# One field of every third tile fetched row by row by SyncE in place of a gather of GpSimd

## The chip, the cores and the metric

The kernel runs on one core of one Trainium2 chip. The metric is the time of one execution on the device, in microseconds (us). The engines are TensorE (PE; its weight loads are PEld), VectorE (DVE), ScalarE (ACT), GpSimd (POOL) and SyncE (SP). The kernel before takes 558.92 us, the median of three runs (558.09 to 559.47).

## The reference

2048 samples each carry 32 field indices. Every index picks a row of 256 floats from the table of its field. The kernel computes the dot products of all pairs of the 32 rows, appends 16 given numbers, and sends the result through three dense layers.

```python
e = jnp.stack([tbl_0[ids[:, 0]], ..., tbl_31[ids[:, 31]]], axis=1)   # [2048, 32, 256]
dots = jnp.einsum('bnd,bmd->bnm', e, e)
z = dots[:, iu, ju]                                # 496 pairs i < j
h = jnp.concatenate([z, dense_ctx], axis=1)        # 512 features
h = jnp.maximum(h @ W_top1 + b_top1, 0.0)          # 512 -> 512
h = jnp.maximum(h @ W_top2 + b_top2, 0.0)          # 512 -> 256
y = h @ W_top3                                     # 256 -> 1
```

The 12 largest tables have 12500 rows, the others 1250 or 1000. All is float32.

## The kernel before

The samples go in 16 tiles of 128, numbered 0 to 15. For six of the small fields (1000 rows each) a row is looked up by TensorE, as a product of a one-hot matrix with a table that is kept on the core (`look_up`, L346). The row numbers for these arrive by `load_ids` (L251, issued by SP), DVE makes the one-hot matrices (`make_one_hot`, L725), and each look-up serves two tiles. There are three such look-ups in each step of one tile.

The other 26 fields are gathered. They stand in 13 pairs per tile, called units; tile 0 has two more units, since half of its looked-up fields are gathered too. For each unit POOL issues two indirect DMAs (`gather`, L303), each of which reads 128 rows of 1 KB by a list of 128 row numbers. They land in one of nine places of the ring `rows` (`PLACES = 9`); before a gather POOL waits for `turn_done`, which says that the unit nine earlier was turned. TensorE turns a unit (`turn`, L330): it waits for `gathered[place]`, transposes the four 128x128 blocks into a bank of PSUM, and ACT or DVE copies them into `turned`.

A step of tile t on TensorE begins with `turn_all(t)`: units 4 to 12 of the tile, with `turn_features(t - 1)` (L412, it raises `ft_done`) after unit 6, and then the first layer of the tile before (L427). It goes on with `gram(t, k)` (L368) in eight parts, between which stand the parts of the look-ups, the second layer of the tile before (L448) and the first four units of tile t + 1. Unit 12, the last of a tile, is thus the last that TensorE turns ahead of the tile's products, and it holds fields 30 and 31 of the kernel's own numbering.

SP issues the plain loads in program order. After the loads of the start it runs one loop turn per tile: three `load_ids`, each behind a wait for `one_hot_made` (a ring of three buffers), and one `load_dense` behind a wait for `ft_done`. An instruction that waits on SP holds all that stands behind it.

The last tile has its own products (`last_gram`, L389), and after them come the last layers and the output of 2048 numbers (L291).

Of the kernel before, what the change touches and what calls it, by code (L numbers as in the profile page):

```python
# [35 lines left out]
    return np.array(order)  # L36


def dlrm_tower(nc, dense_ctx, ids, small_ids, tables, w1, b1, w2, b2, w3, out):
    fp32 = mybir.dt.float32  # L40
    fp32r = mybir.dt.float32r
    int32 = mybir.dt.int32
# [23 lines left out]
        BEGIN.append(len(UNITS))  # L66

    PLACES = 9

    ACT_UNITS = [0, 2, 4, 6, 8, 10, 12]  # L70
    RING = 4
# [42 lines left out]
    with ctx:  # L114
# [6 lines left out]
        def sem(name):  # L121
            return ctx.enter_context(nc.semaphore(name))
# [40 lines left out]
        late_h2 = turn_ps[1]  # L163

        weighted = area[:, 3 * FEATURES:3 * FEATURES + HIDDEN2]

        y_rows = area[0:TILES, 0:P]

# [9 lines left out]
        dense_in = sem("dense_in")  # L178
        weights_in = sem("weights_in")
        table_in = [sem(f"table_in{i}") for i in range(SMALL)]  # L180
        gathered = [sem(f"gathered{i}") for i in range(PLACES)]
        row_numbers_ready = sem("row_numbers_ready")
        ident_zero = sem("ident_zero")
# [50 lines left out]

        def n_gathered(n):

            return 16 * sum(len(UNITS[m][1]) for m in range(n % PLACES, n + 1, PLACES))

        def n_ids(n):

# [4 lines left out]
        @block.sync  # L245
        def _(sp):
            def load_ids(n):
                f, t, tiles = LOOKUPS[n]
                if n >= IDS_RING:
                    sp.wait_ge(one_hot_made, n - IDS_RING + 1)  # L250
                sp.dma_start(ids_across[:, n % IDS_RING, 0:tiles * P],  # L251
                             small_ids[f, t * P:(t + tiles) * P].partition_broadcast(P),
                             ).then_inc(ids_across_in[n % IDS_RING], 16)

            def load_table(i):
                table = tables[i].rearrange("(p r) d -> p r d", r=SUB)
                sp.dma_start(landed[0:SP_WIDE, i, :, 1, :], table[0:SP_WIDE, :, :]).then_inc(table_in[i], 16)
                sp.dma_start(landed[SP_WIDE:SP, i, :, 1, :], table[SP_WIDE:SP, :, :]).then_inc(table_in[i], 16)

            def load_dense(t):  # L260
                if t > 0:
                    sp.wait_ge(ft_done, t)
                sp.dma_start(features[:, PAIRS:FEATURES], dense_ctx[t * P:(t + 1) * P, :]).then_inc(dense_in, 16)

            sp.dma_start(row_ids[:, 0, :], ids[:, 0, :]).then_inc(row_ids_in[0], 16)
# [12 lines left out]
            sp.dma_start(w3_sb[:, :], w3.rearrange("n a -> (a n)").partition_broadcast(P)).then_inc(weights_in, 16)  # L278
            sp.dma_start(b1_sb[:, :], b1).then_inc(weights_in, 16)
            sp.dma_start(b2_sb[:, :], b2.partition_broadcast(P)).then_inc(weights_in, 16)  # L280
            for c in range(KC):
                sp.dma_start(w1_sb[:, c, :], w1[c * P:(c + 1) * P, :]).then_inc(weights_in, 16)
            load_ids(5)
            for t in range(TILES):
                if t + 2 in FIRST:
                    for n in range(FIRST[t + 1], FIRST[t + 2]):
                        load_ids(n)
                if t + 1 < TILES:
                    load_dense(t + 1)
            sp.wait_ge(y_kept, 1)  # L290
            sp.dma_start(out.rearrange("(t p) a -> t (p a)", p=P), y_rows).then_inc(y_out, 16)  # L291
            sp.wait_ge(y_out, 16)

        @block.gpsimd
        def _(pool):
            def gather(n):
# [2 lines left out]
                    pool.wait_ge(row_ids_in[t], 16)  # L299
                if n >= PLACES:  # L300
                    pool.wait_ge(turn_done, n - PLACES + 1)
                for j, f in enumerate(unit):
                    pool.indirect_dma_start(  # L303
                        out=rows[:, n % PLACES, j, :], out_offset=None, in_=tables[f],
                        in_offset=bass.IndirectOffsetOnAxis(ap=row_ids[:, t, f:f + 1], axis=0),
                    ).then_inc(gathered[n % PLACES], 16)
# [10 lines left out]
        @block.tensor  # L317
        def _(pe):
            def turn(n):
                _, unit = UNITS[n]  # L320
# [6 lines left out]
                for c in range(CHUNKS):  # L327
                    for j in range(len(unit)):
                        at = (c * len(unit) + j) * P
                        last = pe.transpose(turn_ps[n % RING][:, at:at + P],  # L330
                                            rows[:, n % PLACES, j, c * P:(c + 1) * P], ident[:, :])
                last.then_inc(turn_done, 1)

            def look_up(n, first, end):
# [454 lines left out]
```

## Time and profile before

| | us |
|---|---|
| median of three runs | 558.92 |
| the profiled execution's own time | 555.82 |
| its span on the core | 554.0 |
| PE busy (matmul) | 507.0 (92%) |
| POOL busy | 397.3 (72%) |
| DVE busy | 250.0 (45%) |
| ACT busy | 184.0 (33%) |

The profile shows one execution. Busy time counts instructions that work on an engine; the issue of a DMA by SP, a wait or an instruction on registers does not count. For POOL the time between two instructions in which it waits for nothing that the profile shows appears as "issue", so that an engine can be the limit with a share far under 100%. TensorE's mean granted clock was 0.988 of full speed.

### The profile page before, as it was taken

Reading aid. Unit: us, or ns where it says so; the run is one execution under the profiler, and the core shown is the slowest. Engines: PE = TensorE matmul, PEld = TensorE weight load, DVE = VectorE, ACT = ScalarE, POOL = GpSimd, SP = SyncE. Lnnn points to the kernel's source line nnn. Section 1 sums busy time; section 2 is a strip of 40 time slices with the busy share of each in tenths; the row PEclk is TensorE's granted clock in tenths of the full one; section 3 lists DMA queues with packets and bytes.
Section 4 is the critical chain, followed back from the end, with each engine's and each line's share of the span. In section 5 each row is a group of like instructions: output and inputs, shape, how many; then the busy total and the mean of one; then the engine's idle time right before and its main releaser. Section 6 shows DMA issues by size and latency. Waiting matters only on the chain.

```text
span 554.0 us, 24236 instructions
## 1 busy us (share of the span) xinstructions
PE 507.0 (92%) x11015; PEld 467.2 (84%) x11015; DVE 250.0 (45%) x592; ACT 184.0 (33%) x355; POOL 397.3 (72%) x426
## 2 busy tenths in 40 slices
PE   0775999999899999989998998999899998999987
PEld 0775899999799899979997988898789997899986
DVE  3674562634446264443626335362633636244232
ACT  1785160513306051230605124060511505142242
POOL 6777767777777777777777777777777777777710
PEclk9997999999899999999999999999999999999999
DMA  8999434444444434444444445444444443433310
GB/s 196 267 261 310 146 99 127 117 118 116 128 119 117 128 112 126 117 125 117 119 124 117 119 118 127 118 118 129 116 119 117 127 117 113 114 111 107 109 38 2
DMA packets 37459, 70.97 MB, mean 128 GB/s; under 512 B 10382, under 2 KB 23438, under 8 KB 37358
## 3 DMA queue, kind: packets, MB, share of 16 engines
q0 software_dynamic: 20112, 54.95, 35.3%
q1 hardware_dynamic: 17246, 14.48, 10.8%
q8 instruction: 87, 1.43, 1.0%
q14 instruction: 14, 0.11, 0.1%
HBM read 69.39 MB, written 0.01 MB: 125 GB/s over the span
## 4 chain that ended last, share of the span: by engine, by line
PE 79%; DMA 8%; POOL 6%; issue 4%; ACT 2%; DVE 1%; DVEq 0%
PE look_ps L346 32%; PE quad_ps L368 16%; PE top_ps L427 9%; DMA rows<-in_tbl,row_ids 7%; PE turn_ps L330 6%; PE quad_ps L330 6%; POOL rows L303 6%; PE top_ps L448 5%; PE quad_ps L389 1%; PE top_ps L412 1%; ACT area L542 1%; ACT products L536 1%; PE turn_ps L427 1%; DVE one_hot L725 0%; DVE turned L653 0%
## 5 line engine op out<-in xcount | busy, mean ns | idle before, releaser
L303 POOL DMA_INDIRECT rows<-in_tbl,row_ids x419 | 396.5, 946 | 131.1 <-issue 116.7
L346 PE MATMUL look_ps<-one_hot,small 125*128 125x256 f32 (+1 forms) x1536 | 222.0, 294 | 7.9 <-DVE small L715 6.8
L346 PEld LDWEIGHTS look_ps<-one_hot,small 125*128 125x128 f32 x1536 | 196.4, 194 | 11.7 <-issue 9.6
L725 DVE TENSOR_SCALAR one_hot<-ids_across,sub_row 125x256 fp32r<-125x256 int32 (+1 forms) x384 | 118.3, 378 | 118.4 <-PE look_ps L346 112.3
L368 PE MATMUL quad_ps<-turned 128*32 128x31 f32 x7680 | 103.4, 199 | 1.3 <-issue 1.2
L368 PEld LDWEIGHTS quad_ps<-turned 128*32 128x32 f32 x7680 | 86.0, 110 | 20.8 <-issue 1.6
L521 ACT ACTIVATE ahead<-look_ps 128x512 f32<-128x512 f32 (+1 forms) x48 | 28.0, 584 | 202.6 <-PE look_ps L346 202.6
L330 PE MATMUL turn_ps<-ident,rows 128*128 128x128 f32 x424 | 63.5, 282 | 24.6 <-DMA rows<-in_tbl,row_ids 23.5
L330 PEld LDWEIGHTS turn_ps<-ident,rows 128*128 128x128 f32 x424 | 47.4, 143 | 29.5 <-issue 15.1
L330 PE MATMUL quad_ps<-ident,rows 128*128 128x128 f32 x414 | 62.0, 282 | 8.6 <-DMA rows<-in_tbl,row_ids 8.3
L512 ACT ACTIVATE turned<-turn_ps 128x512 f32<-128x512 f32 x57 | 36.0, 632 | 67.0 <-PE quad_ps L368 42.6
L330 PEld LDWEIGHTS quad_ps<-ident,rows 128*128 128x128 f32 x414 | 46.4, 143 | 13.2 <-DMA rows<-in_tbl,row_ids 9.9
L427 PE MATMUL top_ps<-area,w_sb 128*128 128x128 f32 x448 | 53.7, 279 | 0.0
L427 PEld LDWEIGHTS top_ps<-area,w_sb 128*128 128x128 f32 x448 | 52.6, 196 | 0.0
L512 ACT ACTIVATE turned<-quad_ps 128x512 f32<-128x512 f32 x55 | 34.8, 633 | 44.0 <-PE quad_ps L368 39.2
L669 DVE STREAM_TRANSPOSE products<-quad_ps 128x992 f32<-128x992 f32 x15 | 18.3, 1217 | 60.0 <-PE quad_ps L368 60.0
L653 DVE COPY turned<-turn_ps 128x512 f32<-128x512 f32 x49 | 33.5, 683 | 13.0 <-PE turn_ps L330 13.0
L706 DVE TENSOR_TENSOR top_ps<-top_ps,b_sb 128x256 f32<-128x256 f32 x14 | 6.0, 432 | 71.1 <-PE top_ps L448 71.1
L653 DVE COPY turned<-quad_ps 128x512 f32<-128x512 f32 (+1 forms) x49 | 33.1, 675 | 9.9 <-PE quad_ps L330 9.9
L581 ACT ACTIVATE area<-top_ps,b_sb 128x128 f32<-128x128 f32 x56 | 16.0, 368 | 36.4 <-PE top_ps L427 36.4
L448 PE MATMUL top_ps<-w_sb,area 128*128 128x256 f32 x112 | 27.9, 392 | 0.0
L531 ACT ACTIVATE turned<-ahead 128x768 f32<-128x768 f32 x16 | 25.5, 1593 | 0.0
(64 smaller groups left out, 192.2 us busy)
## 6 DMA issues: line engine op xcount, KB each, us to landing
rows<-in_tbl,row_ids POOLq DMA_INDIRECT x419
ids_across<-in_small_ids SPq DMA_DIRECT2D x45, 128.0 KB, 3.4
landed<-in_tbl SPq DMA_DIRECT2D x6, 896.0 KB
w_sb<-in_W_top SPq DMA_DIRECT2D x4, 256.0 KB, 9.8
landed<-in_tbl SPq DMA_DIRECT2D x6, 104.0 KB
w_sb<-in_W_top SPq DMA_DIRECT2D x1, 512.0 KB, 13.7
area<-in_dense_ctx SPq DMA_DIRECT2D x16, 8.0 KB
row_ids<-in_ids SPq DMA_DIRECT2D x1, 240.0 KB, 13.3
```

The costliest lines, as they stand in the source:

```text
L303: pool.indirect_dma_start(out=rows[:, n % PLACES, j, :], out_offset=None, in_=tables[f], in_offset=bass.IndirectOffsetOnAxis(ap=row_ids[:, ...
L330: last = pe.transpose(turn_ps[n % RING][:, at:at + P], rows[:, n % PLACES, j, c * P:(c + 1) * P], ident[:, :])
L346: last = pe.matmul(look_ps[:, c * width:(c + 1) * width], small[:, f, r, part, c * P:(c + 1) * P], one_hot[n % 2][:, r, 0:width], start=(r ...
L368: last = pe.matmul(gram_ps[q * FIELDS:(q + 1) * FIELDS, g // BANK_GROUPS, at:at + COLS], turned[:, c, s, :], turned[:, c, s, 0:COLS], star ...
L427: last = pe.matmul(bank[:, m * P:(m + 1) * P], w1_sb[:, c, m * P:(m + 1) * P], turned_features[:, c, :], start=(c == 0), stop=(c == KC - 1))
L448: last = pe.matmul(bank[:, 0:HIDDEN2], hidden[:, c, :], w2_sb[:, c, :], start=(c == 0), stop=(c == M1 - 1))
L512: act.activation(turned[:, :, :, f:f + len(unit)], turn_ps[n % RING][:, 0:CHUNKS * len(unit) * P].rearrange("p (c f s) -> p c s f", c=CHUN ...
L521: act.activation(ahead[:, f, :, 0:tiles * P], look_ps[:, 0:CHUNKS * tiles * P].rearrange("p (c s) -> p c s", c=CHUNKS), ACT.Copy).then_inc ...
L531: act.activation(turned[:, :, :, fs].rearrange("p c s f -> p f c s"), ahead[:, fs, :, half * P:(half + 1) * P], ACT.Copy).then_inc(act_pla ...
L653: dve.tensor_copy(turned[:, :, :, f:f + len(unit)], turn_ps[n % RING][:, 0:CHUNKS * len(unit) * P].rearrange("p (c f s) -> p c s f", c=CHU ...
L669: dve.transpose(square[:, 0:COLS, 0:FIELDS], grams).then_inc(unfolded, 1)
L725: last = dve.tensor_scalar(one_hot[n % 2][:, r, 0:width], ids_across[0:SP, n % IDS_RING, 0:width], sub_row[:, r:r + 1], None, ALU.is_equal)
```

## The change

The tiles 3, 6, 9, 12 and 15 (`ROW_TILES`) no longer have field 31 (`ROW_FIELD`) gathered by POOL. `pool_fields(n)` leaves it out of unit 12 of these tiles, and the counts of `gathered` follow. SP fetches it instead, into a fixed 256 columns of `area` (`row_field`): `fetch_rows` reads 16 row numbers from memory into registers, and then issues 16 transfers of one row of 1 KB each, with the address from a register. Eight such groups make a tile's 128 rows. They stand in SP's program between the loads of three loop turns, at most three groups in a turn, one after each `load_ids`. The first group of a fetch waits for the turn of unit 12 of the tile that used the buffer before; there is one buffer. TensorE's turn of unit 12 of such a tile waits for `rows_in[i]` as well, and takes the second field from `row_field`. A new input `row_list` holds field 31's row numbers in a line.

```diff
+    ROW_FIELD = FIELDS - 1
+    ROW_UNIT = len(PAIRED) - 1
+    ROW_EVERY = 3
+    ROW_TILES = list(range(ROW_EVERY, TILES, ROW_EVERY))
+    ROWS_AT_ONCE = 16
+    ROW_GROUPS = P // ROWS_AT_ONCE
+    GROUPS_AFTER = 3
...
+        row_field = area[:, 3 * FEATURES + HIDDEN2:3 * FEATURES + HIDDEN2 + D]
...
+        def pool_fields(n):
+
+            t, unit = UNITS[n]
+            return [f for f in unit if f != ROW_FIELD or t not in ROW_TILES]
...
+            def fetch_rows(i, group):
+                t = ROW_TILES[i]
+                if group == 0 and i > 0:
+                    sp.wait_ge(turn_done, BEGIN[ROW_TILES[i - 1]] + ROW_UNIT + 1)
+                at = t * P + group * ROWS_AT_ONCE
+                _, numbers = nc.values_load_multi_w_load_instructions(
+                    row_list[0:1, at:at + ROWS_AT_ONCE], engines=[mybir.EngineType.SP],
...
+                for k, number in enumerate(numbers):
+                    p = group * ROWS_AT_ONCE + k
+                    sp.dma_start(row_field[p:p + 1, :], tables[ROW_FIELD][bass.ds(number, 1), :],
+                                 ).then_inc(rows_in[i], 16)
...
-                if t + 2 in FIRST:
-                    for n in range(FIRST[t + 1], FIRST[t + 2]):
-                        load_ids(n)
+                made = range(FIRST[t + 1], FIRST[t + 2]) if t + 2 in FIRST else range(0)
+                for k in range(GROUPS_AFTER):
+                    if k < len(made):
+                        load_ids(made[k])
+                    group = t % ROW_EVERY * GROUPS_AFTER + k
+                    if t < ROW_TILES[-1] and group < ROW_GROUPS:
+                        fetch_rows(t // ROW_EVERY, group)
                 if t + 1 < TILES:
                     load_dense(t + 1)
...
-                for j, f in enumerate(unit):
+                for j, f in enumerate(pool_fields(n)):
...
+                if len(pool_fields(n)) < len(unit):
+                    pe.wait_ge(rows_in[ROW_TILES.index(t)], 16 * P)
```

On SP, in the loop turn of tile 3, there stood the dense load and then the three loads of row numbers one behind another (before):

```order
30 L251 DMA ids_across<-in_small_ids 128x256 [waits one_hot_made] x3
31 L263 DMA area<-in_dense_ctx 128x16 [waits ft_done]
32 L251 DMA ids_across<-in_small_ids 128x256 [waits one_hot_made] x3
```

Now, at the same place, the first of these loads is followed by a group of tile 6's fetch. `in_row_list_ptr` is the address of the list, `in_row_list` the 16 numbers; an ISA row multiplies a row number up to an address, and the DMA behind it moves that row:

```order
315 L278 DMA area<-in_dense_ctx 128x16 [waits ft_done]
316 L266 DMA ids_across<-in_small_ids 128x256 [waits one_hot_made]
317 L285 TENSOR_LOAD in_row_list_ptr [waits turn_done]
318 L285 REGISTER_ALU
319 L285 TENSOR_LOAD in_row_list
320 L291 ISA
321 L291 DMA area<-in_tbl 1x256
```

Between the load in row 316 and the next `load_ids` there are now a wait for `turn_done`, two register loads, one register instruction, and 16 pairs of an ISA instruction and a DMA.

On POOL, at the end of tile 3 and the beginning of tile 4, the list of gathers ran on from table 30 to 31 (before):

```order
114 L303 DMA rows<-in_tbl_29,row_ids 128x256
115 L303 DMA rows<-in_tbl_30,row_ids 128x256 [waits turn_done]
116 L303 DMA rows<-in_tbl_31,row_ids 128x256
117 L303 DMA rows<-in_tbl_0,row_ids 128x256 [waits turn_done]
118 L303 DMA rows<-in_tbl_1,row_ids 128x256
```

And it now goes from table 30 to tile 4's first gather:

```order
114 L336 DMA rows<-in_tbl_29,row_ids 128x256
115 L336 DMA rows<-in_tbl_30,row_ids 128x256 [waits turn_done]
116 L336 DMA rows<-in_tbl_0,row_ids 128x256 [waits turn_done]
117 L336 DMA rows<-in_tbl_1,row_ids 128x256
118 L336 DMA rows<-in_tbl_3,row_ids 128x256 [waits turn_done]
```

Every gather behind it has moved up by one position, and the same happens at the four other tiles.

## Rows read from the trace of the kernel before

**Rows 1.** The page: busy us (share) x instructions of each engine.

```profile
PE 507.0 (92%) x11015; PEld 467.2 (84%) x11015; DVE 250.0 (45%) x592; ACT 184.0 (33%) x355; POOL 397.3 (72%) x426
```

**Rows 2.** Waits of all engines: engine line, releaser, us in total, times, longest us.

```profile
POOL rows L303 <- issue: 116.7, 383, 0.3
...
PE turn_ps L330 <- DMA rows<-in_tbl,row_ids: 23.5, 8, 12.2
...
POOL rows L303 <- PE quad_ps L330: 8.7, 20, 2.9
```

**Rows 3.** Timeline of POOL at its one long gap and at its end.

```profile
start us, us, engine line op out<-in xcount [idle before <-releaser]
...
70.50 0.94 POOL L303 DMA_INDIRECT rows<-in_tbl,row_ids  x1 [0.30 <-issue]
74.32 0.94 POOL L303 DMA_INDIRECT rows<-in_tbl,row_ids  x1 [2.87 <-PE quad_ps L330]
...
525.78 0.94 POOL L303 DMA_INDIRECT rows<-in_tbl,row_ids  x1 [0.30 <-issue]
527.02 0.94 POOL L303 DMA_INDIRECT rows<-in_tbl,row_ids  x1 [0.30 <-PE turn_ps L330]
528.27 0.94 POOL L303 DMA_INDIRECT rows<-in_tbl,row_ids  x1 [0.30 <-issue]
```

**Rows 4.** Windows of three tiles each: length, busy (x count) per engine, PE clock, DMA.

```profile
171.80:269.30 97.50, 94.70 (x2123) 87.05 (x2122) 44.70 (x106) 30.54 (x65) 73.75 (x78) 1.00 0.44 120
366.90:464.40 97.50, 94.67 (x2125) 87.23 (x2124) 45.13 (x107) 30.54 (x63) 73.75 (x78) 1.00 0.44 121
```

**Rows 5.** Timeline of PE: first and last of six waits for unit 12, then the end.

```profile
142.27 0.96 PE L330 MATMUL turn_ps<-ident,rows 128*128 128x128 f32 x4 [2.14 <-DMA rows<-in_tbl,row_ids]
...
239.82 0.66 PE L330 MATMUL turn_ps<-ident,rows 128*128 128x128 f32 x4 [2.21 <-DMA rows<-in_tbl,row_ids]
...
467.35 0.66 PE L330 MATMUL quad_ps<-ident,rows 128*128 128x128 f32 x4 [2.13 <-DMA rows<-in_tbl,row_ids]
...
528.68 0.66 PE L330 MATMUL turn_ps<-ident,rows 128*128 128x128 f32 x4 [0.45 <-DMA rows<-in_tbl,row_ids]
...
531.00 0.66 PE L330 MATMUL turn_ps<-ident,rows 128*128 128x128 f32 x4 [0.77 <-DMA rows<-in_tbl,row_ids]
```

**Rows 6.** The chain that ended last, its end: start us, us, what.

```profile
527.02 0.94 POOL rows L303
527.97 0.30 issue
528.27 2.68 DMA rows<-in_tbl,row_ids
530.95 0.04 issue
531.00 0.67 PE turn_ps L330 x4
```

**Rows 7.** Timeline of SP (SPq): its issues in the first three steps of the pattern.

```profile
137.98 0.33 SPq L263 DMA_DIRECT2D area<-in_dense_ctx  x1
138.35 0.43 SPq L251 DMA_DIRECT2D ids_across<-in_small_ids  x1
...
144.18 0.33 SPq L251 DMA_DIRECT2D ids_across<-in_small_ids  x1
...
172.94 0.33 SPq L263 DMA_DIRECT2D area<-in_dense_ctx  x1
173.31 0.44 SPq L251 DMA_DIRECT2D ids_across<-in_small_ids  x1
...
204.20 0.33 SPq L263 DMA_DIRECT2D area<-in_dense_ctx  x1
```

**Rows 8.** Waits of SP's queue: line, releaser, us in total, times, longest us.

```profile
SPq L263 <- PE top_ps L412: 231.6, 15, 29.4
SPq L251 <- DVE one_hot L725: 229.7, 29, 13.9
```

**Rows 9.** SP's other issues: at the start, in the crowded start phase, at the end.

```profile
34.59 0.70 SPq L263 DMA_DIRECT2D area<-in_dense_ctx  x1
...
46.70 4.24 SPq L251 DMA_DIRECT2D ids_across<-in_small_ids  x3
...
552.25 0.36 SPq L291 DMA_DIRECT2D out_y<-area  x1
```

**Rows 10.** DMA issues: out<-in engine op xcount, KB each, median us to landing.

```profile
ids_across<-in_small_ids SPq DMA_DIRECT2D x45, 128.0 KB, 3.4
...
row_ids<-in_ids SPq DMA_DIRECT2D x1, 16.0 KB, 1.8
...
out_y<-area SPq DMA_DIRECT2D x1, 8.0 KB, 1.4
```

**Rows 11.** Timeline of DVE: the one-hot that uses the load issued at 138.35.

```profile
163.45 2.44 DVE L725 TENSOR_SCALAR one_hot<-ids_across,sub_row 125x256 fp32r<-125x256 int32 x8 [5.05 <-PE look_ps L346]
```

**Rows 12.** DMA queues: packets, MB, share of 16 engines over the span.

```profile
q0 software_dynamic: 20112, 54.95, 35.3%
q1 hardware_dynamic: 17246, 14.48, 10.8%
```

More of the change, by code:

```diff
@@ L36, in pair_order, with dlrm_tower @@
     return np.array(order)
-def dlrm_tower(nc, dense_ctx, ids, small_ids, tables, w1, b1, w2, b2, w3, out):
+def dlrm_tower(nc, dense_ctx, ids, small_ids, row_list, tables, w1, b1, w2, b2, w3, out):
     fp32 = mybir.dt.float32
@@ L180, in dlrm_tower @@
         table_in = [sem(f"table_in{i}") for i in range(SMALL)]
+        rows_in = [sem(f"rows_in{i}") for i in range(len(ROW_TILES))]
         gathered = [sem(f"gathered{i}") for i in range(PLACES)]
@@ L235, in n_gathered @@
         def n_gathered(n):
-            return 16 * sum(len(UNITS[m][1]) for m in range(n % PLACES, n + 1, PLACES))
+            return 16 * sum(len(pool_fields(m)) for m in range(n % PLACES, n + 1, PLACES))
+        def pool_fields(n):
+            t, unit = UNITS[n]
+            return [f for f in unit if f != ROW_FIELD or t not in ROW_TILES]
         def n_ids(n):
@@ L263, in load_dense @@
                 sp.dma_start(features[:, PAIRS:FEATURES], dense_ctx[t * P:(t + 1) * P, :]).then_inc(dense_in, 16)
+            def fetch_rows(i, group):
[5 more added lines that the diff above has]
+                    row_list[0:1, at:at + ROWS_AT_ONCE], engines=[mybir.EngineType.SP],
+                    min_val=0, max_val=tables[ROW_FIELD].shape[0] - 1,
+                    skip_runtime_bounds_check_because="row numbers of this table, as for the gathers")
+                for k, number in enumerate(numbers):
+                    p = group * ROWS_AT_ONCE + k
+                    sp.dma_start(row_field[p:p + 1, :], tables[ROW_FIELD][bass.ds(number, 1), :],
+                                 ).then_inc(rows_in[i], 16)
             sp.dma_start(row_ids[:, 0, :], ids[:, 0, :]).then_inc(row_ids_in[0], 16)
@@ L319, in turn @@
             def turn(n):
-                _, unit = UNITS[n]
+                t, unit = UNITS[n]
                 pe.wait_ge(gathered[n % PLACES], n_gathered(n))
+                if len(pool_fields(n)) < len(unit):
+                    pe.wait_ge(rows_in[ROW_TILES.index(t)], 16 * P)
                 if n >= RING:
@@ L329, in turn @@
                         at = (c * len(unit) + j) * P
+                        field = rows[:, n % PLACES, j, :] if unit[j] in pool_fields(n) else row_field
                         last = pe.transpose(turn_ps[n % RING][:, at:at + P],
-                                            rows[:, n % PLACES, j, c * P:(c + 1) * P], ident[:, :])
+                                            field[:, c * P:(c + 1) * P], ident[:, :])
                 last.then_inc(turn_done, 1)
@@ L776 @@
     laid["small_ids"] = np.ascontiguousarray(by_slot[:, :SMALL].T)
+    laid["row_list"] = np.ascontiguousarray(by_slot[:, FIELDS - 1].reshape(1, BATCH))
     laid["ids"] = np.ascontiguousarray(by_slot.reshape(TILES, P, FIELDS).transpose(1, 0, 2))
@@ L784 @@
     out = nc.dram_tensor("out_y", (BATCH, 1), mybir.dt.float32, kind="ExternalOutput").ap()
-    dlrm_tower(nc, aps["dense_ctx"], aps["ids"], aps["small_ids"], [aps[f"tbl_{f}"] for f in SLOTS],
+    dlrm_tower(nc, aps["dense_ctx"], aps["ids"], aps["small_ids"], aps["row_list"], [aps[f"tbl_{f}"] for f in SLOTS],
                aps["W_top1"], aps["b_top1"], aps["W_top2"], aps["b_top2"], aps["W_top3"], out)
```

## The prediction, made before the changed kernel had run

> **What bounds the kernel now.** By the page's first part alone TensorE would be the limit: 92% busy, POOL 72% [rows 1]. So I read the table of waits next, to see what each engine waits for. POOL's idle time is nearly all "issue": 383 gaps, none over 0.3 us [rows 2]. POOL is thus never idle for a reason outside itself; a gather costs it 0.95 us of busy time and 0.30 us behind it, 1.25 us in all. The timeline of POOL confirms this: one gap of 2.87 us at 71 us, and from 74.32 to 528.27 us one gather each 1.25 us. Where a gap names TensorE as the releaser it is 0.30 us as well, so nothing was really waited for [rows 3]. The windows of three tiles say the same: 78 gathers (26 a tile) in 97.5 us [rows 4], which is 78 x 1.25, or 32.5 us a tile.
>
> TensorE could go faster. SP's dense load is released once a tile by TensorE (by `ft_done`), so its times show TensorE's step: from 172.94 to 204.20 us it is 31.26 us, and where TensorE waits, from 137.98 to 172.94, it is 34.96 [rows 7]. The waits are for unit 12, which needs a tile's last gather: six of them between 142 and 468 us, 1.71 to 2.21 us each and 12.3 us in sum, then 0.45 and 0.77 us at the end [rows 5]; together 13.5 us. The chain of the end goes through POOL's last gather (528.27 us), its landing (530.95) and the turn [rows 6]. What stands behind that turn takes 23 us whatever went before.
>
> So POOL sets the time from 74 us on, and TensorE has 13.5 us in hand against it. SP, which gets the new work, waits for 461 us of the span [rows 8].
>
> **The change part by part.**
>
> *What POOL loses.* Five gathers, 5 x 1.25 = 6.25 us. All lie behind the gap at 71 us and before the last gather, so the last one starts 6.25 us earlier, if POOL is not held. Three tiles then take POOL 77 x 1.25 = 96.25 us against TensorE's 3 x 31.26 = 93.8 us: POOL stays the bound, and TensorE has to give up only 6.25 of its 13.5 us of waiting. The end follows: -6.25 us. What could take some back is the ring of nine places, since POOL comes 1.25 us nearer to TensorE at each such tile; today it is not really held behind 74.32 us. I take 0 for this and keep 0 to +1 us for the range.
>
> *What TensorE gains or loses.* The same four transposes per unit, two from another buffer: 0. One more wait, for `rows_in`, at unit 12 of five tiles. Behind it on TensorE stand the first layer of the tile before and the tile's products, and through `turn_done` POOL's ring: a late row stops everything. It costs nothing as long as SP is done in time, so SP decides.
>
> *What SP gets.* Per fetched tile 8 groups; a group is two register loads, one register instruction, and 16 times an ISA instruction with a DMA. The trace of before has none of them but plain DMAs, so each is bounded:
>
> A DMA from SP: 0.33 us, with 0.04 us to the next (137.98 + 0.33 against 138.35), so 0.37 us from below [rows 7]. The output with only 16 rows took 0.36, the dense load in the crowded start phase 0.70 [rows 9], which gives 0.74 from above. The address step before it: at least one such gap of 0.04 us, at most POOL's gap of 0.30 [rows 3]. For both together I take 0.48 us, which is what a load costs right behind another (0.44 + 0.04) [rows 7]; the ends are 0.41 and 1.04. Sixteen: 7.7 us (6.6 to 16.6).
>
> A register load has to fetch from memory and come back. No row shows one. From below it is a gap, 0.04 us; the nearest rows are the shortest whole transfers, 1.4 us for 8 KB and 1.8 us for 16 KB [rows 10]. I take 1.4 us each, 2.8 a group (0.1 to 3.6).
>
> A group is then 10.5 us, with ends of 6.7 and 20.
>
> *What SP can afford.* For tile 6 the first group waits for the turn of tile 3's unit 12 (ends at 143.2), and the last row must have landed before tile 6's unit 12 (239.82) [rows 5]. That is 96.6 us, less 1.25 for the missing gather, less nine plain loads in between at about 0.4 us, less 1.8 us for the last landing: 90 us, or 11.2 us a group. For tile 3 the groups begin behind the second of the three loads at 46.70 us [rows 9], at about 48, and must be there before 142.27 less 1 us, which leaves 10.9 us a group. My 10.5 lies under both, by 4 to 6% only. Under the limit the fetch costs nothing; above it every us more a group costs 8 us a tile, 40 us in all.
>
> *What is queued behind the groups on SP.* The loads of row numbers: one issued at 138.35 us serves a one-hot that starts at 163.45 [rows 11] and lands 3.4 us after its issue [rows 10], so it may come 21 us late at no cost. It comes at most two groups late. The dense load has a whole step. So 0 for both, while SP keeps up over three tiles.
>
> *The DMA engines.* 17246 packets of SP's queue took 10.8% of 16 engines [rows 12], 56 ns each. 640 more of at most that size are 36 us of one engine at worst, 6% of the span; gathers could land some 0.1 to 0.5 us later where they meet. During the last step no row is fetched any more, so the last landing keeps its time. 0, up to +0.4.
>
> **The Trainium skill against my price.** *Runtime: NRT & Kernel Launch*, section "Instruction fetch mechanics", says that a register load costs about 200 ns for each register, also in bulk. By this a group's 18 registers would be an estimated 3.6 us in place of my 2.8, and the sum would come out at about no change. No run here shows it yet; my sum goes by the rows.
>
> **Sum.** -6.25, with 0 to +1 taken back, from an own time of 555.82 us: 549.6 us. The median of the runs shown lies 3.1 us above this execution; so 558.92 - 6.2 = 552.7 us.
>
> **Rivals.**
>
> *SP becomes the bound.* At 0.57 us a row and 2.8 us of register loads, a group is 12 us: tile 3 is late by 8 x 1.1, the four others by 8 x 0.8 each, 34 us together, and the time is 552.7 + 34 = about 587 us; at 13 us a group about 627. It decides from 11.2 us a group on. For it: the limit is near, no row shows a DMA with an address from a register, and the row that I took for the pair holds no address step. Against: SP's idle 461 us [rows 8] are more than 40 x 10.5 = 420.
>
> *SP just misses.* Two register loads at the upper end, 1.8 us each, make a group 11.3 us: 8 x 0.4 for tile 3 and 4 x 8 x 0.1 are 6 us, and the gain is gone: 558.7 us. This is where the page's figure would put it too.
>
> *The ring or the landings take half.* POOL is held by a place at some tiles, or the fetches delay unit 12's landing so that TensorE runs out of what it has in hand: about 3 us left of the gain, 556 us. Against: the windows show POOL at full rate with PE under 95 of 97.5 us [rows 4].
>
> *The transfers don't overlap,* each row taking its 1.4 us alone: 128 rows are 179 us against 90, and the time would nearly double. Against: the load at 138.35 is issued while the one at 137.98 cannot have landed. I count it in the first rival's chance.
>
> **How the numbers follow.** Forecast 0.60 (own range 551.5 to 554), half the gain 0.05, just missed 0.08, SP the bound 0.27. A change under 0.3% (1.7 us) can't be told from none here. Faster: 0.60 + 0.05 = 0.65; same: 0.08; slower: 0.27. The first three hold 0.73; to reach 0.80 the range takes in a quarter of the SP case, up to 11.9 us a group: 552.7 + 40 x 0.73 = 582 us. Below, 6.25 us is all that the removed gathers hold, and 1.2 us are left for the spread of runs: 551.5.
>
> **What would show it.** Right: POOL's gathers still 1.25 us apart from about 74 us on, 414 of them, the last near 522 us; turns of unit 12 at tiles 3, 6, 9, 12 and 15 that wait, if at all, for the gather; SP's groups under 11 us with idle time left at the end of each third turn. Wrong: TensorE waiting many us for `area` at these turns, POOL's gaps behind them growing with TensorE as the releaser, and SP's DMAs standing end to end over all three turns. Then the price of a row or of the register loads is the term that failed, and SP's timeline shows which. A gain well under 6 us with SP on time would mean that POOL was held by the ring.

## The result, and the profile after

The changed kernel took 550.37 us (median of 4 runs, 549.18 to 551.41) against 558.50 us for the kernel before in the same measurement: ratio 0.9867, 95% interval 0.9834 to 0.9900. Forecast were 552.7 us and a range from 551.5 us, so the direction is right and the time lies 1.1 us under the range's low end. Three later series of the same program gave 551.7 to 552.1 us (ratios 0.9895 to 0.9905, below), inside the range. Executions that ran in a slower state are left out of the times and ratios below: two of `groups8`, and one of `seven_tiles` that took 1576.31 us.

The busy line of the page, which answers to [rows 1], loses POOL's five gathers (426 to 421 instructions) and 4 us of POOL's time; PE is busy 4.3 us less, with the same 11015 matmuls:

```profile
PE 502.7 (92%) x11015; PEld 463.4 (85%) x11015; DVE 249.3 (46%) x592; ACT 184.0 (34%) x355; POOL 393.2 (72%) x421
```

The waits of all engines (line, releaser, us in total, times, longest us) answer to [rows 2]. Behind its restart at 73 us POOL still stands for nothing but its own 0.3 us. No line says that TensorE waited for `area`, where SP's rows land, and none of TensorE's at a turn stands under "issue", as such a wait does in `groups8` below:

```profile
POOL rows L336 <- issue: 115.5, 379, 0.3
...
PE turn_ps L366 <- DMA rows<-in_tbl,row_ids: 21.2, 8, 11.2
...
POOL rows L336 <- PE quad_ps L366: 7.5, 20, 1.7
```

POOL's timeline, as in [rows 3]: the one long gap, one gather in the middle, and the last.

```profile
start us, us, engine line op out<-in xcount [idle before <-releaser]
...
70.43 0.94 POOL L336 DMA_INDIRECT rows<-in_tbl,row_ids  x1 [0.30 <-issue]
73.05 0.94 POOL L336 DMA_INDIRECT rows<-in_tbl,row_ids  x1 [1.68 <-PE quad_ps L366]
...
215.66 1.08 POOL L336 DMA_INDIRECT rows<-in_tbl,row_ids  x1 [0.30 <-issue]
217.05 0.95 POOL L336 DMA_INDIRECT rows<-in_tbl,row_ids  x1 [0.30 <-issue]
...
521.45 0.95 POOL L336 DMA_INDIRECT rows<-in_tbl,row_ids  x1 [0.30 <-PE turn_ps L366]
```

From the restart to the last gather POOL needs 521.45 - 73.05 = 448.40 us, before 528.27 - 74.32 = 453.95: 5.55 us less, where five gathers are 6.25. The row at 215.66 shows where 0.7 us went: now and then a gather takes up to 1.08 us instead of 0.95 (ten over 0.96 us behind the restart, two before the change). The restart itself is 1.27 us earlier, and from the last gather to the end it is 25.95 us (before 25.73). Together: -5.55 - 1.27 + 0.22 = -6.6, the whole difference of the two spans (554.0 and 547.4).

Two windows of three tiles answer to [rows 4]; they are 96.25 us long here, 77 gathers:

```profile
171.80:268.05 96.25, 93.97 (x2119) 86.39 (x2118) 45.37 (x108) 30.71 (x62) 73.00 (x77) 1.00 0.44 121
268.05:364.30 96.25, 93.87 (x2115) 86.44 (x2113) 43.98 (x106) 29.19 (x60) 72.81 (x77) 1.00 0.45 122
```

SP's timeline answers to [rows 7]. It shows DMAs only; register loads and address steps are what lies between them:

```profile
start us, us, engine line op out<-in xcount [idle before <-releaser]
238.96 6.50 SPq L291 DMA_DIRECT2D area<-in_tbl  x16
245.51 0.37 SPq L266 DMA_DIRECT2D ids_across<-in_small_ids  x1
248.89 6.80 SPq L291 DMA_DIRECT2D area<-in_tbl  x16
255.75 0.36 SPq L266 DMA_DIRECT2D ids_across<-in_small_ids  x1
```

Sixteen rows take 6.50 us, 0.41 us a row. From the end of the plain load at 245.88 to the first row at 248.89 are 3.01 us: the two register loads. From the first register load to the last row, over the 40 groups the median is 9.9 us (9.45 to 10.73). The waits of SP's queue were 231.6 and 229.7 us [rows 8] and are now:

```profile
SPq L278 <- PE top_ps L448: 44.1, 5, 10.9
...
SPq L266 <- DVE one_hot L761: 4.5, 2, 4.2
SPq L285 <- PE turn_ps L366: 3.5, 2, 1.8
SPq L285 <- PE quad_ps L366: 3.5, 2, 1.8
```

SP is nearly full, but not the bound: a dense load still waits for TensorE, and the four waits on L285, for the turn of unit 12 (1.79 us each), say that SP stood ready for the next tile's rows before their place was free. The queues, against [rows 12]:

```profile
q0 software_dynamic: 19872, 54.29, 35.6%
q1 hardware_dynamic: 18526, 15.14, 11.3%
```

SP's queue has 1280 packets more for 640 rows: each row goes as one packet of 1 KB and one of 4 bytes. The chain's end answers to [rows 6]; it goes through the landing of the last gather but one (issued at 520.20) and its turn. From the first of the last tile's products (525.70) to the end are 21.7 us, as before (532.34 to 554.0):

```profile
520.20 2.78 DMA rows<-in_tbl,row_ids
522.98 0.04 issue
523.02 0.66 PE turn_ps L366 x4
```

### The profile page after: what moved, and what is told of

Same layout as the page of the kernel before. It is cut to its first block, busy times and chain, and to the rows that moved or that the text cites. A ratio compares the mean times of both kernels' runs of the same rounds, so it can differ in the third digit from the quotient of the medians.

```text
span 547.4 us, 26273 instructions
## 1 busy us (share of the span) xinstructions
PE 502.7 (92%) x11015; PEld 463.4 (85%) x11015; DVE 249.3 (46%) x592; ACT 184.0 (34%) x355; POOL 393.2 (72%) x421
## 3 DMA queue, kind: packets, MB, share of 16 engines
q1 hardware_dynamic: 18526, 15.14, 11.3%
## 4 chain that ended last, share of the span: by engine, by line
PE 59%; POOL 22%; issue 9%; DMA 7%; DVE 2%; ACT 1%; POOLq 0%; DVEq 0%
PE look_ps L382 23%; POOL rows L336 22%; PE quad_ps L404 12%; PE top_ps L463 7%; DMA rows<-in_tbl,row_ids 6%; PE quad_ps L366 5%; PE turn_ps L366 5%; PE top_ps L484 4%; PE quad_ps L425 1%; PE top_ps L448 1%; DVE turned L689 1%; PE turn_ps L463 1%; ACT area L578 0%; DVE one_hot L761 0%; PE turn_ps L484 0%
## 5 line engine op out<-in xcount | busy, mean ns | idle before, releaser
L336 POOL DMA_INDIRECT rows<-in_tbl,row_ids x414 | 392.4, 948 | 128.4 <-issue 115.5
L463 PE MATMUL top_ps<-area,w_sb 128*128 128x128 f32 x448 | 52.3, 275 | 0.0
L463 PEld LDWEIGHTS top_ps<-area,w_sb 128*128 128x128 f32 x448 | 51.1, 192 | 0.0
L705 DVE STREAM_TRANSPOSE products<-quad_ps 128x992 f32<-128x992 f32 x15 | 18.2, 1217 | 62.8 <-PE quad_ps L404 62.8
L689 DVE COPY turned<-turn_ps 128x512 f32<-128x512 f32 x49 | 33.6, 685 | 11.1 <-PE turn_ps L366 11.1
```

Of the source, the lines that this page charges most:

```text
L336: pool.indirect_dma_start(out=rows[:, n % PLACES, j, :], out_offset=None, in_=tables[f], in_offset=bass.IndirectOffsetOnAxis(ap=row_ids[:, ...
L463: last = pe.matmul(bank[:, m * P:(m + 1) * P], w1_sb[:, c, m * P:(m + 1) * P], turned_features[:, c, :], start=(c == 0), stop=(c == KC - 1))
L689: dve.tensor_copy(turned[:, :, :, f:f + len(unit)], turn_ps[n % RING][:, 0:CHUNKS * len(unit) * P].rearrange("p (c f s) -> p c s f", c=CHU ...
L705: dve.transpose(square[:, 0:COLS, 0:FIELDS], grams).then_inc(unfolded, 1)
```

## The experiments

Theory A: POOL is the bound; five gathers less are -6.25 us; SP costs nothing up to 11.2 us a group and 40 us per us above. Its rivals: the gain is something else than the gathers, or SP's transfers give back or hide part of it. Each series was timed with the kernel before on the same chip (its medians 556.5 to 557.9 us).

**The changed kernel again** (no edit).

> The changed kernel once more, for the size of the gain. Theory A (the gain is POOL's list, five gathers of 1.25 us, and the rest of the first measurement is the spread of runs): 6.25 us under the kernel before, a ratio of 0.989. Theory B (the change also gives something beside the five gathers): 8 us under it, a ratio of 0.9855. In the trace both expect the five gathers' 6.25 us between the gap of POOL near 71 us and its last gather; under A what is left over differs from the first run's, under B it is there again at the same place.

Measured 552.05 us (551.34 to 553.17), ratio 0.9899 (0.9877 to 0.9921). A second repeat was timed with a later series:

> The changed kernel once more, as it is. Theory A: the gathers give -6.25 us and SyncE's transfers take 0.65 us back, -5.6 us in all; the further 1 to 2 us by which the first measurement was lower came from where the half-clock stretches fell in those few executions: 552.2 us against 557.8, ratio 0.990, with 0.987 to 0.992. Rival: the change gives 8 us, as in the first measurement: ratio 0.9855.

Measured 551.73 us, ratio 0.9905 (0.9881 to 0.9929). So the gain is 5 to 6 us, and the 8 us of the first measurement were not met again, though its interval (0.9834 to 0.9900) overlaps with these. The rows of POOL in the second repeat:

```profile
70.42 0.95 POOL L336 DMA_INDIRECT rows<-in_tbl,row_ids  x1 [0.30 <-issue]
75.41 0.94 POOL L336 DMA_INDIRECT rows<-in_tbl,row_ids  x1 [4.04 <-PE quad_ps L366]
...
523.60 0.95 POOL L336 DMA_INDIRECT rows<-in_tbl,row_ids  x1 [0.30 <-issue]
```

523.60 - 75.41 = 448.19 us (448.29 in the first repeat), the same as the 448.40 above. What differs from one execution to the next lies outside this stretch. The restart comes at 75.22 and 75.41 us in the repeats, against 73.05, and the end lies 27.89 and 27.80 us behind the last gather, against 25.95. In the first repeat these are 2.17 and 1.94 us, nearly all of the 4.0 us between the two spans (551.4 and 547.4). Its chain shows how the end became longer:

```profile
492.24 3.92 DMA rows<-in_tbl,row_ids
496.20 0.66 PE turn_ps L366 x4
496.85 5.20 PE top_ps L463 x32
```

Behind this wait, the one for tile 14's unit 12, no gather stands in the chain any more: TensorE ran the first layer in 5.20 us where it takes 3.57 in the other steps (granted clock 0.69 from 495 to 500 us, in the first profile 1.00), and reached the last turns after the last rows had landed. So over the last step TensorE set the time there, and not POOL. Windows of the start phase (length, busy of PE, PEld, DVE, ACT, POOL, granted clock, DMA, GB/s), first of the changed kernel's first profile, then of the first repeat:

```profile
36.00:46.00 10.00, 7.07 (x57) 6.29 (x56) 4.12 (x7) 4.79 (x8) 7.56 (x9) 1.00 1.09 252
46.00:56.00 10.00, 3.95 (x79) 3.61 (x79) 8.08 (x18) 8.51 (x11) 7.56 (x9) 0.66 1.04 344
```

```profile
36.00:46.00 10.00, 9.67 (x70) 9.46 (x70) 5.35 (x10) 6.74 (x8) 7.57 (x9) 0.83 1.07 249
46.00:56.00 10.00, 3.65 (x81) 3.16 (x79) 7.03 (x16) 8.24 (x10) 7.56 (x9) 0.69 1.08 287
```

The profile of the first measurement had the granted clock at full speed from 36 to 46 us, the repeat at 0.83, as had the kernel before. That fits a TensorE that is later there and a later restart, but the run `fetch_only` below also has 0.83 and restarts at 73.54 us. What sets the restart within these 2.4 us stays open, and so does why the clock fell in some executions and not in others.

**Only the cut.** POOL's five gathers go, nothing is fetched by SP (the buffer is filled once with other rows).

```diff
-                for j, f in enumerate(unit):
+                for j, f in enumerate(pool_fields(n)):
...
+            def fetch_once():
+                sp.dma_start(row_field, tables[ROW_FIELD][0:P, :]).then_inc(rows_in[0], 16)
```

> POOL's five gathers are left out as in the change, but SP fetches no rows: row_field is filled once, by one plain load of the table's first 128 rows, so field 31 of the tiles 3, 6, 9, 12 and 15 is not what the ids ask for. Theory A: the same time as the changed kernel to within 1 us, since SP's fetch was hidden whole. Theory B (the row transfers cost something where they meet the gathers, some tenths of a us at every third tile): 1 to 2 us under the changed kernel.

Measured 551.12 us, ratio 0.9886 (0.9858 to 0.9914): 0.9 us under the repeat in the same series, which is within theory A and not clear of the spread. POOL's rows:

```profile
75.45 0.94 POOL L323 DMA_INDIRECT rows<-in_tbl,row_ids  x1 [4.04 <-PE quad_ps L353]
...
523.11 0.94 POOL L323 DMA_INDIRECT rows<-in_tbl,row_ids  x1 [0.30 <-PE quad_ps L353]
```

447.66 us, 6.29 less than before: five gathers at 1.25 us, to 0.04 us.

**Only the fetch.** SP fetches and TensorE waits, but POOL gathers everything.

```diff
-            return [f for f in unit if f != ROW_FIELD or t not in ROW_TILES]
+            return unit
...
-                if len(pool_fields(n)) < len(unit):
+                if ROW_FIELD in unit and t in ROW_TILES:
```

> SP fetches the rows as in the change and TensorE waits for them at the same turns, but POOL gathers all fields as before and TensorE takes its rows from there: the fetch's cost alone. Theory A: as the kernel before to within 1 us (ratio 0.998 to 1.002); SP's groups are 9.9 us as in the changed kernel, under the limit of about 11.3 (no gather less, so the window is 97.5 us). Theory B: 1 to 2 us over the kernel before.

Measured 557.89 us, ratio 1.0006 (0.9987 to 1.0025).

```profile
73.54 0.94 POOL L336 DMA_INDIRECT rows<-in_tbl,row_ids  x1 [2.00 <-PE quad_ps L366]
...
528.17 0.95 POOL L336 DMA_INDIRECT rows<-in_tbl,row_ids  x1 [0.30 <-issue]
```

454.63 us, 0.68 more than before. The two halves add up: -6.29 + 0.68 = -5.61, and the change shows -5.55 to -5.76. So the gain is the cut, and SP's transfers cost POOL some 0.65 us by lengthening single gathers. That 0.7 us is too small for the timed ratios; it rests on one trace of each kernel.

**Groups of 8 rows,** for SP more register loads for as many rows.

```diff
-    ROWS_AT_ONCE = 16
+    ROWS_AT_ONCE = 8
...
-    GROUPS_AFTER = 3
+    GROUPS_AFTER = 6
```

> The change with groups of 8 rows in place of 16 (16 groups a tile, six in a loop turn), so that SP loads registers twice as often: the price of an SP that is too slow. From the changed kernel's trace a register load pair is 3.0 us and a row 0.41 us; if a pair for 8 numbers costs 2.7 to 3.0 us, a tile's fetch is 128 x 0.41 + 16 x 2.85 = 98 us against about 79 now, and with the plain loads, the last landing and the turn about 104 us from one such turn to the next, against 96.3 for POOL. Theory A (SP decides from the point at which its fetch no longer fits in three tiles, and then at the full rate): tile 3 late by some 9 us and four more cycles by 8 each, about 40 us over the changed kernel, 590 us; rival (TensorE's 13.5 us in hand and the ring of nine places take up most of it): under 570 us.

Measured 569.7 us (median of four, 566.37 to 573.30), ratio 1.022 (1.0172 to 1.0268): slower, but 20 us less than theory A's 590, and just inside the rival's "under 570". A group took 5.57 us: its two register loads took 2.3 us, not the 2.7 to 3.0 that the 590 were worked out from (8 numbers 0.9 us, half of 16's 1.8). So 16 rows took 11.1 us, which the prediction's limit of 11.2 would have let go free. The waits, of an execution of 575.95 us, show that SP set the pace already. PE's wait at the turn for `area` is called "issue"; there is one at each of the five served tiles, of 2.8 to 8.5 us, and POOL is held behind them:

```profile
POOL rows L336 <- PE quad_ps L366: 22.8, 20, 6.1
PE turn_ps L366 <- issue: 16.3, 4, 8.5
```

SP itself stood 20.2 us on L266, for the row-number places that VectorE had not read yet.

**A dearer group, 16 rows.** A first try, with a second load whose numbers nothing used, kept exactly the instructions of the changed kernel (26273), as SP's groups of 9.96 us show:

> The change with one more register load (an address pair and eight numbers that nothing uses) in each group of 16, so that a group takes about 12.1 us instead of 9.9; the rest is untouched. Theory A (above 11.2 us a group SyncE sets the time, and each us over it costs 40 us: 8 groups for each of 5 tiles): 8 x (12.1 - 11.2) = 7.2 us late per tile, 36 us in five tiles, less the 5.6 us that the left-out gathers give: about 588 us, 580 to 596; SyncE no longer waits at its ring in the middle, and TensorE waits for the rows at unit 12 of tiles 3, 6, 9, 12 and 15. Rival (TensorE's hand and the buffers ahead of it take most of the lateness, GpSimd goes on ahead): under 570 us. Second rival (the time is that of GpSimd whatever SyncE takes): 552 us.

It was thus a third repeat: 551.79 us, ratio 0.9895 (0.9864 to 0.9926). In the second try the loaded numbers were used:

```diff
+                _, again = nc.values_load_multi_w_load_instructions(
+                    row_list[0:1, at:at + ROWS_AT_ONCE // 2], engines=[mybir.EngineType.SP],
...
-                for k, number in enumerate(numbers):
+                for k, number in enumerate(again + numbers[ROWS_AT_ONCE // 2:]):
```

> The change with a second register load in each group (an address and eight numbers), whose numbers are used for the group's first eight rows, so that it stays in the program: a group takes 9.9 + 2.1 = 12.0 us. Theory A, the prediction's price (free up to 11.2 us a group, 40 us per us above it): 40 x 0.8 = 32 us more than the change, about 584 us. Theory B (the room is smaller than 11.2, since SyncE also stands some 3 to 8 us in each cycle at its ring and at unit 12, as the 8-row groups showed: 16 groups of 5.57 us, 89 us, made a cycle of 101 us, so 12 us go to everything else): a cycle is 8 x 12.0 + 12 = 108 us instead of 96.25, five times 11.7, less what the first tile has in hand: 600 us and more. Rival (TensorE and the buffers take most of the lateness): under 570 us.

Measured 586.5 us, ratio 1.0522 (1.0487 to 1.0558). SP's timeline, then the waits:

```profile
367.26 6.51 SPq L295 DMA_DIRECT2D area<-in_tbl  x16
373.83 0.37 SPq L266 DMA_DIRECT2D ids_across<-in_small_ids  x1
379.12 6.46 SPq L295 DMA_DIRECT2D area<-in_tbl  x16
```

```profile
PE turn_ps L370 <- issue: 28.4, 3, 13.2
POOL rows L340 <- PE quad_ps L370: 26.7, 24, 10.4
POOL rows L340 <- PE turn_ps L370: 20.4, 21, 6.7
```

From the end of the plain load (374.20) to the last row (385.58) this group takes 11.4 us; the median of all is 11.9. The time is 34.6 us over the repeats' 551.9. Theory A's 584 us was met to 2.5 us; theory B's 600 us fell, and so did the rival that TensorE takes most of the lateness. If the prediction's 40 us per us is taken as given, the limit is 11.9 - 34.6/40 = 11.0 us a group, where the prediction had 11.2 (10.9 for tile 3). One run can't show limit and slope apart. The 8-row groups, 11.1 us for 16 rows, cost 17.8 us, more than this slope gives; SP stood 20.2 us at L266 there and 6.4 us here.

**A cheaper group.** The list lies in one partition of core memory, so that its register load needs no address pair.

```diff
-                    row_list[0:1, at:at + ROWS_AT_ONCE], engines=[mybir.EngineType.SP],
+                    list_sb[P - 1:P, at:at + ROWS_AT_ONCE], engines=[mybir.EngineType.SP],
...
+            sp.dma_start(list_sb[P - 1:P, :], row_list[:, :]).then_inc(list_in, 16)
...
```

> The change with row_list loaded once into a free partition of the core's memory, so that a group needs one register load of 16 numbers from there and no load of the list's address. Theory A (SP's fetch is hidden whole while it fits, so its length is worth nothing): the time of the changed kernel to within 1 us (551 to 553 us); the loads of a group fall from 3.0 us to 1.9 us or less and SP shows more idle time. Rival (the register loads from memory are what slows POOL's gathers by 0.65 us in sum): 0.6 us faster, with POOL's gathers exactly 1.25 us apart again.

Measured 553.07 us, ratio 0.9917 (0.9887 to 0.9947): a group fell to 7.88 us, and the time didn't follow. SP's pace is not what the change waits for. Single gathers were still up to 1.10 us long, so the rival, that the loads from memory lengthen them, fell too. From the restart to the last gather POOL took 450.03 us here; TensorE held it, longest at 429 us, by 0.8 us.

**The same for seven tiles** (3, 5, ..., 15), four groups in each of SP's turns.

```diff
-    ROW_TILES = list(range(ROW_EVERY, TILES, ROW_EVERY))
+    ROW_TILES = list(range(3, TILES, 2))
...
-    GROUPS_AFTER = 3
+    GROUPS_AFTER = 4
...
```

> The same with field 31 fetched for seven tiles (3, 5, 7, 9, 11, 13, 15), four groups in each of two loop turns. POOL loses seven gathers, 8.75 us. Two tiles of 51 gathers are 63.75 us; less six plain loads, the last landing and the start behind the turn there remain about 58 us, 7.3 us a group. Theory A (SP decides from that point, at 8 us of a tile for every us): with 6.5 us for the 16 rows, a register load of 0.8 us or less gives 549 to 550 us; a load of 1.8 us makes a group 8.4 us, six cycles late by 9 us each less the gain, about 600 us. Rival (TensorE and the ring hide part of a late row): under 580 us in the second case.

Measured 586.5 us (median of five), ratio 1.0481 (1.0439 to 1.0523). Two tiles have no room for eight groups of 7.87 us: from the start of one tile's fetch to the next SP needs 68.6 to 70.4 us, for what POOL does in 63.75. The waits, TensorE's for the rows again under "issue":

```profile
POOL rows L343 <- PE turn_ps L373: 26.1, 24, 5.5
POOL rows L343 <- PE quad_ps L373: 23.4, 24, 5.1
PE quad_ps L373 <- issue: 15.9, 4, 6.6
```

**How far POOL can be cut.** The field is left out of POOL's list in tiles 1 to 15, with no fetch; the buffer is filled once, as in the cut alone.

```diff
+    ROW_TILES = list(range(1, TILES))
```

> Field 31 is left out of POOL's list in all tiles from 1 on and row_field is filled once by a plain load, so field 31 of these tiles is not what the ids ask for: how much of POOL's list can go before TensorE is the bound. POOL loses 15 x 1.25 = 18.75 us. Theory A (TensorE had 13.5 us in hand): it becomes the bound, and the gain is 12 to 14 us, 544 to 546 us; TensorE no longer waits for gathers and POOL waits for places. Rival (TensorE's waits were not the whole of what it has in hand): 18 to 19 us, 539 us.

Measured 541.69 us, ratio 0.9709 (0.9688 to 0.9730): 16.1 us less. Tile 1's gathers lie before the restart, so 14 x 1.25 = 17.5 us could count; POOL needs 513.30 - 75.50 = 437.80 us, 16.15 less than before. A window of three tiles:

```profile
174.00:267.75 93.75, 92.79 (x2112) 85.62 (x2111) 44.10 (x106) 29.00 (x61) 70.89 (x76) 1.00 0.44 119
```

PE is busy for 92.79 of 93.75 us. The chain that ended last has no gather in it behind 41 us: TensorE has become the bound here. So it had about 16 us in hand, not the 13.5 that its waits for unit 12 add up to [rows 5]. The time lies between theory A's 544 to 546 us and the rival's 539.

**A better version?** Three kernels serve seven tiles with a cheaper row: VectorE makes byte offsets of the row numbers, so that no address instruction is needed.

```diff
+                                 tables[ROW_FIELD].rearrange("(o r) d -> o (r d)", o=1).bitcast(mybir.dt.uint8)[0:1, bass.ds(number, 4 * D)],
...
+            dve.tensor_scalar(row_bytes[:, :], row_ids[:, :, ROW_FIELD], 4 * D, None, ALU.mult).then_inc(bytes_made, 1)
...
+            sp.dma_start(byte_list.rearrange("o (t p) -> p (o t)", p=P), row_bytes[:, :], allow_slow_non_contiguous=True).then_inc(bytes_out, 16)
```

> The same row fetch, but VectorE turns the row numbers into byte offsets at the start (times 1024), they lie in one partition of core memory, and a transfer adds its offset to a register without the address instruction; seven tiles (3, 5, ..., 15) are served instead of five, four groups in each turn of SyncE. Theory A (the work of GpSimd sets the time as long as SyncE keeps up, and seven gathers at 1.25 us fall away): a group of 16 takes 1.38 us for its load and 16 x 0.335 to 0.37 us, 6.7 to 7.3 us; eight of them and SyncE's other transfers then fit into two tiles (64.3 us), TensorE never waits for the rows, GpSimd gives -8.75 us and about +0.9 is taken back: 549 to 551 us against 557.8, ratio 0.984 to 0.988, GpSimd from its restart near 71 us to its last gather about 446.0 us (453.95 before). Rival: the address instruction runs beside something else anyway, a group stays at 7.8 us as in seven_tiles, and the time is 580 to 590 us. Second rival: the transfers slow GpSimd's gathers more with each tile, and no more than -5.6 us is left: 552 to 553 us.

Measured 556.13 us, ratio 0.9977 (0.9954 to 1.0000). The group was 6.46 us and SP in time, but the start failed:

```profile
75.34 0.95 POOL L350 DMA_INDIRECT rows<-in_tbl,row_ids  x1 [0.30 <-issue]
83.75 0.94 POOL L350 DMA_INDIRECT rows<-in_tbl,row_ids  x1 [7.46 <-PE quad_ps L380]
```

SP stood 15.5 us at the list's store, 2048 packets of four bytes, until they had landed, and the row numbers behind it came late. The second kernel makes the list earlier:

```diff
             load_dense(0)
+            sp.wait_ge(bytes_made, 1)
+            sp.dma_start(byte_list.rearrange("o (t p) -> p (o t)", p=P), row_bytes[:, :], allow_slow_non_contiguous=True).then_inc(bytes_out, 16)
...
```

> As byte_rows (byte offsets made on the chip, 16 rows in 6.46 us as measured there, seven tiles), but the list is made earlier: VectorE multiplies near 28 us instead of 51.5, the 2048 four-byte packets of the list (15.5 us from issue to landing in byte_rows) are issued before the weights, near 40 us, and SyncE waits for them only behind two more transfers of small row numbers, with the first rows fetched in tile 0's last place. Theory A (in byte_rows SyncE stood 18 us at the list, so that the small row numbers came late, TensorE with them, and GpSimd stood 8.4 us at 75.3 us; everything behind it ran at the pace of 1.25 us per gather): GpSimd restarts once, near 75 us, its last gather starts at 522 to 523 us (523.6 in the repeat of the change), and the time is 549.5 to 551 us against 557.5, ratio 0.985 to 0.988; half-clock stretches of TensorE, whose hand is smaller by 2.5 us, may hold GpSimd once by 1 to 2 us. Rival: seven tiles leave TensorE and SyncE no room, late rows and half-clock stretches cost more than 2.5 us, and the time is 552 to 556 us, no better than the change.

Measured 556.82 us, ratio 0.9991 (0.9965 to 1.0016), near the rival's 552 to 556 us, yet not for its reason. The list was now in the way of the load behind it: issuing the first weights took SP 11.53 us, where the same load took 0.82 us in `byte_rows`. That load, and POOL's restart:

```profile
39.45 11.53 SPq L315 DMA_DIRECT2D w_sb<-in_W_top  x1
```

```profile
81.32 0.94 POOL L354 DMA_INDIRECT rows<-in_tbl,row_ids  x1 [7.71 <-PE quad_ps L384]
...
527.80 0.95 POOL L354 DMA_INDIRECT rows<-in_tbl,row_ids  x1 [0.30 <-PE turn_ps L384]
```

527.80 - 81.32 = 446.48 us: the gathers' gain was there, and a restart 7.0 us later than before the change (six later than in the repeats) ate it. The third kernel loads the numbers from `row_list` and moves the list in larger pieces:

```diff
+            sp.dma_start(row_bytes[:, :], row_list.rearrange("o (t p) -> (o t) p", p=P // 2)).then_inc(numbers_in, 16)
...
+                    dve.tensor_scalar(row_bytes[:, :], row_bytes[:, :], 4 * D, None, ALU.mult).then_inc(bytes_made, 1)
...
+            sp.dma_start(byte_list.rearrange("o (t p) -> (o t) p", p=P // 2), row_bytes[:, :]).then_inc(bytes_out, 16)
```

> As byte_rows2 (byte offsets, no address instruction, seven tiles), but the list isn't scattered in four-byte packets: it is loaded as 32 rows of 64 numbers, VectorE multiplies it in one instruction, and it is stored and loaded again in 256-byte and 8 KB pieces. Theory A (the gain goes with the gathers left out, and the start phase of byte_rows2, 81.3 instead of 75.4 us at GpSimd's restart, goes whole into the time): GpSimd restarts near 75 us, its last gather starts 446.5 us later as in byte_rows2 (448.2 in the repeat of the change), near 521.5 us, and the time is 549.5 to 551 us against 557.3, ratio 0.986 to 0.989. Rival: TensorE has too little in hand, late rows and half-clock stretches cost what the two further gathers give, and the time is 552 us or more.

Measured 549.04 us (547.51 to 551.42), ratio 0.9877 (0.9850 to 0.9905).

```profile
73.97 0.94 POOL L356 DMA_INDIRECT rows<-in_tbl,row_ids  x1 [2.69 <-PE quad_ps L386]
...
519.69 0.95 POOL L356 DMA_INDIRECT rows<-in_tbl,row_ids  x1 [0.30 <-PE turn_ps L386]
```

445.72 us, 8.23 less than before, for seven gathers (8.75): the gain goes with the gathers left out, and the fetch takes about 0.1 us a tile back. The load of the first weights took 0.89 us to issue here, though the list, in pieces of 256 bytes, still took 14.0 us to land. The kernel beats the kernel before; against the change (0.9895 to 0.9905 in the three repeats, 0.9867 at first) it is 1 to 2 us faster by the repeats' ratios, but the intervals overlap, so that part isn't settled.

## Why the prediction was right, and which step of it failed

- *POOL is the bound, a gather is 1.25 us, five are 6.25.* Shown from the restart to the last gather: the cut alone gives 6.29 us, and 14 gathers still give 16.15 of 17.5, where TensorE becomes the bound. (The 414 gathers that the prediction counts from 74 us on are those of the whole run; 359 stand behind the restart.)
- *0 to +1 us taken back.* 0 was taken, 0.65 came, inside the bounds, but not from the ring of places that was named for it: the fetch alone lengthens POOL's gathers. By which path isn't shown. The register loads from memory are not it (`list_in_sbuf`).
- *TensorE has 13.5 us in hand.* Under-sized; `cut_15` used 16. The sum counted the waits for unit 12 alone. In `cut_15` the idle time of TensorE in three tiles fell from 2.80 to 0.96 us, and its busy time, too, from 94.70 to 92.79.
- *A group is 16 x 0.48 + 2 x 1.4 = 10.5 us.* Measured 16 x 0.41 + 3.3 = 9.9 in the median. The row was 0.07 us too dear (its lower end, 0.41, was right), the register loads 0.5 too cheap. The Trainium skill, *Runtime: NRT & Kernel Launch*, section "Instruction fetch mechanics", says about 200 ns for each register. The estimate of 3.6 us for a group's loads that I drew from it is 0.3 us above the measured median. The trace doesn't agree that each register costs the same: the pair for an address takes 1.2 us in the median, eight numbers 0.9, sixteen 1.8. "No change", which I had drawn from that figure, followed only with my too dear row.
- *The limit of 11.2 us, above it 40 us per us.* The forecast from both held: 586.5 us in `loads_more2`, where 584 was expected; by the price of 40 the limit is 11.0. `groups8`, at 11.1, cost 17.8 us and not 0 to 4; SP's own waits at the ring of row numbers, 20.2 us there, are what the sum had left out. By 11.0, SP had 1.1 us a group left: the rival to which 0.27 was given stood near.
- *The step that failed is the low end:* "6.25 us is all that the removed gathers hold, and 1.2 us are left for the spread of runs". The gathers held no more, but the first measurement fell 2.3 us below the forecast. What the sum put at nothing, without a row for it, is how the two stretches outside POOL's pace differ between executions: all before 74 us, and the end, which was said to take 23 us "whatever went before". In the profiles of one program (the change and its repeats) POOL's restart lies between 73.05 and 75.41 us and the end 25.95 to 27.89 us behind the last gather. The first profile has the low value of both. Against the profile of before its restart was 1.27 us earlier, and that is the part of the 6.6 us that the gathers don't explain. That it is so in the unprofiled runs isn't shown.
- *What was luck.* The own time was forecast as 549.6 us and the profiled execution took 549.18, but by -5.55 - 1.27 + 0.22 and not by -6.25. The 3.1 us from there to the median were those of one execution of the kernel before; in the first series of the change and its two repeats the median lay 1.2 us above, and 1.1 and 1.5 us below, the profiled execution. The base of 558.92 us was high as well: the medians of the kernel before in the six series go from 556.5 to 558.5 us.

## What to carry to other kernels

Work that goes from the engine that sets the pace to one that waits pays nearly in full, as long as the receiver has the room: here 5.6 of 6.25 us, with 9.9 us a group where about 11 were free, and 11.9 cost 34.6 us. Before trusting a range of 1 us, see how much the start and the end differ between executions of one program: here by 2.4 and 1.9 us. And a list that is written in four-byte packets in the start phase can cost more than what it saves.

## What the runs showed of the hardware that was not expected

- A one-row DMA with its address from a register costs SP 0.41 us with its address step, 0.32 us (16 rows in 5.1 us) with the byte offset ready; eight numbers load in 0.9 us, sixteen in 1.8, and sixteen from core memory in 1.2.
- Each such row is two packets, one of 1 KB and one of 4 bytes (18526 - 17246 = 1280 for 640 rows).
- POOL's gathers become longer by 0.03 to 0.14 us now and then while SP's small transfers run, 0.65 us in 455.
- 2048 four-byte packets landed 15.5 to 18.2 us after their issue in the start phase, and the load of weights queued right behind them took 11.53 us to issue, against 0.82 and 0.89 us elsewhere. The same 8 KB in pieces of 256 bytes took 14.0 us to land.
- Right behind a wait of 1.94 us TensorE ran 32 matmuls in 5.20 us in place of 3.57; the granted clock from 495 to 500 us was 0.69.
